# Attention scores from compact f16 halves in two 32-row passes per head, and a new order of steps

## The chip, the cores and the metric

The kernel runs on one core of a Trainium2 chip. The metric is the device time of one execution in microseconds; the median of 3 runs of the kernel before is 266.65 us (266.59 to 267.42).

## The reference

The input is 8 images of 256 tokens with 128 channels. Each image goes through a convolution-style attention layer, an attention layer with 8 heads of 16 channels, a small feed-forward layer and a mixture of 32 experts, of which each token uses two. The change touches the scores of the second layer. There queries, keys and values are all the same matrix `proj`:

```python
def _attn_quantum(h, theta):
    c = jnp.cos(h + theta)
    cp = jnp.cumprod(c, axis=-1)
    z0 = jnp.prod(c[..., 1:], axis=-1)
    return cp.at[..., 0].set(z0)

h = x.reshape(B, S, H, d)                      # 8 x 256 x 8 heads x 16
proj = _attn_quantum(h, theta_attn).transpose(0, 2, 1, 3)
scores = jnp.einsum('bhsd,bhtd->bhst', proj, proj) / jnp.sqrt(jnp.float32(d))
attn = jax.nn.softmax(scores, axis=-1)
ctx = jnp.einsum('bhst,bhtd->bhsd', attn, proj)
```

## The kernel before

One image is one batch `b` (0 to 7); its 256 tokens are two blocks of 128 partitions. All weights stay in the core's memory. The work of a batch is cut into 43 named steps in six chains: `conv` (first layer), `proj` (normalisation, angles, cosines, product scan, splitting), `attn`, `ffn`, `norm` and `moe`. Every engine runs its own part of each step in one common order, which `run_steps` (L387) makes by sorting a start offset per step (`START`) plus an offset per chain and batch (`CHAIN`). Within an engine all instructions run in that order; across engines they are tied by counting semaphores only. So a wait in one step holds back all later steps of that engine.

Eight banks of the accumulator memory hold matmul results, one for each purpose: `conv_ps`, `attn_ps`, two for the scores (`sc_ps`), `ffn_ps`, two for the hidden layer, `moe_ps`. `moe_transpose` of a batch waits until `moe_output` of the batch before has left `moe_ps` (`s_out_sb`); `attn_transpose` waits in the same way for `attn_combine` of the batch before (`s_z`).

The scores are made in f16 with f32 accuracy by splitting. `proj_split`: GpSimd writes `PA` (L1152, L1153), ScalarE casts it to f16, twice next to each other, as the high half of `LS` (L700), VectorE subtracts to get the low half, again twice (L899), and GpSimd copies both halves in another order to `RS` (L1158, L1160). Each head then has 64 values per token on either side: (high, high, low, low) against (high, low, high, low). `attn_transpose`: TensorE transposes `LS` in eight blocks of two heads into `attn_ps` (L492) and `RS` in eight blocks into bank 0 of the scores (L499); VectorE copies them out to `LT` (L907) and `RT` (two copies of 64 partitions, L912). `RT` has a zeroed half for the other head of a block, so that one matmul over 128 rows gives one head's scores. `attn_scores` of head h (L503 on): TensorE makes two matmuls of 256 columns into bank h % 2 (L509) once the exponential of head h-2 has been taken (`s_prob`); ScalarE takes the exponential of the 512 columns into `EB_` (L707). `attn_context` (L519) of four heads multiplies `EB_` with `PA`, each head writing its own 32 partitions of `attn_ps`.

## Time and profile before

| | |
|---|---|
| median of 3 runs | 266.65 us |
| span of the profiled execution | 265.1 us |
| TensorE busy | 193.9 us, 73% |
| VectorE busy | 174.5 us, 66% |
| ScalarE busy | 132.0 us, 50% |
| GpSimd busy | 126.3 us, 48% |
| mean granted TensorE clock | 0.955 |

The shares are averages over a pipeline that fills, runs full and empties; the stretches differ. The busy time of TensorE includes the ends of pipelined matmuls. The chain that ended last is followed back from the last instruction through what released it. PE is TensorE, PEld its weight loads, DVE VectorE, ACT ScalarE, POOL GpSimd. Except for loads at the start and 128 KB out per batch, nothing moves over DMA.

### The profile page before, as it was taken

To read this page: it belongs to the slowest core of one execution; us is meant where nothing else is said; L and a number is where in the kernel's file an instruction comes from. 1 tells how busy PE (TensorE), PEld (TensorE's weight loads), DVE (VectorE), ACT (ScalarE), POOL (GpSimd) and SP (SyncE) were. 2 spreads that over 40 slices of the span, in tenths; PEclk is the share of its full clock that TensorE was granted. 3 is DMA by queue.
4 is the path that set the end of the run, shared out by engine and by line. 5 is a ranking of instruction groups with operands and counts; after the bars stand their busy time and mean duration, and the time that the engine had idled before them with its cause. 6 is when DMAs were issued, how large, how long until landed. Compare 5 with 4: busy or idle time off the path is not lost.

```text
span 265.1 us, 4762 instructions
## 1 busy us (share of the span) xinstructions
PE 193.9 (73%) x1488; PEld 144.9 (55%) x1488; DVE 174.5 (66%) x580; ACT 132.0 (50%) x276; POOL 126.3 (48%) x321
## 2 busy tenths in 40 slices
PE   3372466649775667998899889859788868597395
PEld 2161253423662445786488668637666747476265
DVE  1333464776858788977888788698767566347323
ACT  2523537457458166646846673855447362412021
POOL 3706798265757568555744743376153161022100
PEclk9999999995979979999999999999999999979869
DMA  3385000000000000000000000000000000000000
GB/s 64 107 162 117 0 1 4 0 1 2 0 0 2 0 1 4 0 2 21 1 2 0 22 0 1 22 0 4 0 22 2 1 19 2 21 0 0 22 0 20
DMA packets 12624, 4.33 MB, mean 16 GB/s; under 512 B 6276, under 2 KB 12472, under 8 KB 12600
## 3 DMA queue, kind: packets, MB, share of 16 engines
q1 hardware_dynamic: 12104, 3.94, 6.4%
q8 instruction: 12, 0.20, 0.3%
q10 hardware_dynamic: 496, 0.09, 0.2%
q14 instruction: 12, 0.10, 0.1%
HBM read 2.98 MB, written 1.05 MB: 15 GB/s over the span
## 4 chain that ended last, share of the span: by engine, by line
PE 38%; DVE 29%; issue 10%; POOL 10%; ACT 9%; DMA 1%; ACTq 1%; POOLq 0%; DVEq 0%
PE hidden_ps L621 9%; PE moe_ps L606 6%; PE ffn_ps L570 4%; POOL rstd L1065 4%; DVE HWT L1007 3%; DVE RT L912 3%; DVE st L765 2%; PE sc_ps L509 2%; PE attn_ps L519 2%; PE hidden_ps L625 2%; PE conv_ps L476 2%; PE conv_ps L441 2%; ACT EB_ L707 1%; DMA bv_b<-in_L_conv_bv 1%; DVE ARG L877 1%
## 5 line engine op out<-in xcount | busy, mean ns | idle before, releaser
L707 ACT ACTIVATE EB_<-sc_ps 128x512 f32<-128x512 f32 x64 | 35.1, 597 | 15.1 <-PE sc_ps L509 14.3
L621 PE MATMUL hidden_ps<-XTT,keys_sb 128*128 128x256 f32 x128 | 40.8, 412 | 2.4 <-DVE HWT L1007 2.4
L747 ACT ACTIVATE HR<-hidden_ps 128x256 f32<-128x256 f32 x64 | 24.4, 384 | 35.7 <-PE hidden_ps L625 35.5
L606 PE MATMUL moe_ps<-val_sb,HWT 128*128 128x128 f32 x256 | 33.9, 277 | 2.6 <-DVE HWT L1007 2.6
L606 PEld LDWEIGHTS moe_ps<-val_sb,HWT 128*128 128x128 f32 x256 | 31.0, 192 | 6.6 <-DVE HWT L1007 3.5
L1007 DVE TENSOR_TENSOR HWT<-hidden_ps,HR 128x256 f32<-128x256 f32 x64 | 25.1, 418 | 12.1 <-ACT HR L747 10.3
L1063 POOL TENSOR_SCALAR var<-mv 128x2 f32<-128x2 f32 x32 | 6.6, 205 | 53.2 <-DVE mv L769 52.7
L509 PE MATMUL sc_ps<-RT,LT 128*128 128x256 f16 x128 | 22.9, 290 | 10.0 <-ACT EB_ L707 4.6
L621 PEld LDWEIGHTS hidden_ps<-XTT,keys_sb 128*128 128x128 f32 x128 | 20.6, 202 | 9.3 <-DVE HWT L1007 4.6
L1065 POOL TENSOR_TENSOR rstd<-var,minushalf 128x2 f32<-128x2 f32 x32 | 22.3, 697 | 2.7
L509 PEld LDWEIGHTS sc_ps<-RT,LT 128*128 128x128 f16 x128 | 10.7, 102 | 19.8 <-issue 13.6
L519 PE MATMUL attn_ps<-EB_,PA 128*32 128x256 f32 x256 | 18.1, 403 | 3.2 <-ACT EB_ L707 3.1
L570 PE MATMUL ffn_ps<-w2T_sb,HID 128*128 128x128 f32 x128 | 18.5, 306 | 2.3 <-ACT HID L730 2.3
L570 PEld LDWEIGHTS ffn_ps<-w2T_sb,HID 128*128 128x128 f32 x128 | 17.5, 219 | 3.0 <-ACT HID L730 2.9
L625 PE MATMUL hidden_ps<-WT,spread 96*128 96x256 f16 x64 | 18.1, 283 | 0.8 <-DVE WT L998 0.8
L730 ACT ACTIVATE HID<-ffn_ps 128x512 f32<-128x512 f32 x16 | 9.6, 598 | 8.9 <-PE ffn_ps L563 8.9
L683 ACT ACTIVATE EA<-conv_ps,nmx 128x256 f32<-128x256 f32 x16 | 7.4, 470 | 9.8 <-DVE nmx L836 9.7
L519 PEld LDWEIGHTS attn_ps<-EB_,PA 128*32 128x32 f32 x256 | 6.9, 113 | 9.8 <-ACT EB_ L707 5.6
L912 DVE COPY RT<-sc_ps 64x1024 f16<-64x1024 f16 x16 | 11.1, 694 | 0.3
L775 DVE TENSOR_SCALAR XTK<-T,mv,rstd 128x128 f32<-128x128 f32 x16 | 4.9, 345 | 9.2 <-POOL rstd L1065 9.2
L673 ACT COPY HW<-conv_ps 128x256 f32<-128x256 f32 x8 | 3.0, 372 | 16.0 <-DVE FGs L824 16.0
L476 PE MATMUL conv_ps<-HW,ETs 128*128 128x128 f32 x64 | 9.8, 300 | 1.4 <-DVE ETs L843 1.4
(174 smaller groups left out, 449.0 us busy)
## 6 DMA issues: line engine op xcount, KB each, us to landing
X<-in_x SPq DMA_DIRECT2D x8, 128.0 KB, 7.9
out<-OB SPq DMA_DIRECT2D x8, 128.0 KB, 1.8
keys_sb<-in_L_ffn_keys SPq DMA_DIRECT2D x1, 512.0 KB, 7.8
val_sb<-in_L_ffn_values SPq DMA_DIRECT2D x1, 512.0 KB, 9.0
w_sb<-in_L_attn_W SPq DMA_DIRECT2D x1, 256.0 KB, 2.8
g_b<-in_L_attn_ln_g SPq DMA_DIRECT2D x2, 64.0 KB, 5.5
be_b<-in_L_attn_ln_b SPq DMA_DIRECT2D x2, 64.0 KB, 6.5
bv_b<-in_L_conv_bv ACTq DMA_DIRECT2D x1, 64.0 KB, 3.6
```

The lines of the kernel that those rows point to most:

```text
L476: last = mm(conv_ps[:, t * C:(t + 1) * C], ETs[:, b % 2, m, t * P:(t + 1) * P], HW[:, b % 2, m, :], start=(m == 0), stop=(m == TB - 1))
L509: last = mm(sc_ps[h % 2][:, t * N:(t + 1) * N], LT[:, h // 2, t * P:(t + 1) * P], RT[:, h % 2, h // 2, :], start=True, stop=True)
L519: last = mm(attn_ps[32 * j:32 * j + 32, g * N:(g + 1) * N], PA[:, b % 2, t, h, :], EB_[:, h, t, :], start=(t == 0), stop=(t == TB - 1))
L570: last = mm(ffn_ps[:, t * C:(t + 1) * C], HID[:, k, t * P:(t + 1) * P], w2T_sb[:, k, :], start=(k == 0), stop=(k == FB - 1))
L606: last = mm(moe_ps[:, t * C:(t + 1) * C], HWT[:, k % 4, t * P:(t + 1) * P], val_sb[:, k, :], start=(k == 0 and t == 0), stop=(k == EB - 1) ...
L621: mm(hidden_ps[i][:, 0:N], keys_sb[:, k * EPB:(k + 1) * EPB, :].rearrange("p e h -> p (e h)"), XTT[:, b % 2, :], start=True, stop=True)
L625: mm(hidden_ps[i][:, N:2 * N], spread[:, k, :], WT[:, b % 2, :], start=True, stop=True).then_inc(s_moe_ps, 1)
L707: fn(EB_[:, h, :, :].rearrange("p t n -> p (t n)"), sc_ps[h % 2][:, :], ACT.Exp, scale=1.0 / math.sqrt(DK)).then_inc(s_prob, 1)
L747: fn(HR[:, k % 4, :], hidden_ps[i][:, 0:N], ACT.Relu).then_inc(s_relu, 1)
L912: V.tensor_copy(RT[q, i, :, :].rearrange("p j n -> p (j n)"), b16(sc_ps[0], F16)[q, :]).then_inc(s_RT, 1)
L1007: V.tensor_tensor(HWT[:, k % 4, :], hidden_ps[i][:, N:2 * N], HR[:, k % 4, :], ALU.mult).then_inc(s_hw, 1)
L1065: G.tensor_tensor(rstd[:, which, b, :], var[:, which, b, :], minushalf[:, :], ALU.pow).then_inc(rs, 1)
```

## The change

`LS` and `RS` become `HL` and `LH`: each head has (high, low) and (low, high), 32 values per token, with nothing held twice. ScalarE's cast and VectorE's subtraction write half as much; GpSimd makes `LH` from `HL` by one copy with the halves reversed. Four heads fit a transpose, so eight transposes make both sides, all into `attn_ps`; one copy brings them to `HLT`. `RT`, its zeros, its two copies and the use of score bank 0 for transposes are gone.

A head's scores are now two accumulated passes over 32 rows: (high, low) against (high, low), then (high, low) against (low, high). `attn_pair` handles two heads: its eight matmuls alternate between the heads, which lie in neighbouring groups of 32 rows and write to the two banks. The pair starts once both exponentials of the pair before are taken; the two heads' score semaphore steps come with the seventh and eighth matmul. The four products of halves (high-high, low-low, high-low, low-high) are the same as before.

`START` and `CHAIN` give way to `ORDER`, the place of each step and batch in a sequence of 312 steps. `moe_spread` counts one event less on `s_zeroed`.

```diff
--- before.py
+++ after.py
-START = {
-    "conv_transpose": 0.000, "conv_project": 0.131, "conv_stack": 0.478, "conv_scores": 0.664, "conv_turn": 0.991,
-    "conv_output": 1.190,
-    "proj_norm": 0.000, "proj_angle": 0.375, "proj_reduce": 0.557, "proj_cos": 0.794, "proj_split": 1.014,
-    "attn_transpose": 0.000, "attn_scores0": 0.123, "attn_scores1": 0.129, "attn_scores2": 0.267,
-    "attn_scores3": 0.295, "attn_context0": 0.465, "attn_scores4": 0.494, "attn_scores5": 0.508,
-    "attn_scores6": 0.552, "attn_scores7": 0.608, "attn_context1": 0.762, "attn_turn": 0.852, "attn_back": 1.085,
-    "attn_combine": 1.209,
-    "ffn_norm": 0.000, "ffn_angle": 0.372, "ffn_cos": 0.622, "ffn_transpose": 0.911, "ffn_hidden0": 1.301,
-    "ffn_hidden1": 1.545, "ffn_output": 1.730,
-    "norm_second": 0.000, "norm_third": 0.386,
-    "moe_transpose": 0.000, "moe_select": 0.095, "moe_topk": 0.125, "moe_spread": 0.395, "moe_pair0": 0.535,
-    "moe_pair1": 0.716, "moe_pair2": 0.998, "moe_pair3": 1.157, "moe_output": 1.189,
-}
-
-
-
-CHAIN = {
-    "conv": (0.000, 4.654, 5.883, 7.128, 8.599, 9.969, 11.330, 12.652),
-    "proj": (4.213, 6.104, 7.449, 8.826, 10.191, 11.562, 12.928, 14.505),
-    "attn": (5.828, 7.430, 8.902, 10.276, 11.607, 12.925, 14.284, 15.872),
-    "ffn": (7.444, 8.943, 10.284, 11.705, 13.063, 14.512, 16.131, 17.455),
-    "norm": (9.557, 10.883, 12.224, 14.018, 15.617, 16.569, 18.277, 19.630),
-    "moe": (10.535, 11.888, 13.236, 14.828, 16.048, 17.547, 18.900, 20.600),
+ORDER = {
+ORDER = {
+    "conv_transpose": (0, 8, 21, 38, 61, 85, 125, 163),
+    "conv_project": (1, 9, 22, 39, 66, 87, 128, 169),
+    "conv_stack": (2, 13, 27, 43, 71, 98, 136, 175),
+    "conv_scores": (3, 14, 28, 46, 72, 101, 139, 184),
+    "conv_turn": (4, 17, 31, 50, 75, 108, 148, 194),
+    "conv_output": (5, 19, 34, 55, 81, 110, 158, 199),
+    "proj_norm": (6, 20, 45, 56, 88, 111, 159, 208),
+    "proj_angle": (7, 26, 48, 69, 106, 115, 172, 214),
+    "proj_reduce": (10, 30, 54, 92, 117, 118, 188, 223),
+    "proj_cos": (11, 33, 59, 93, 121, 152, 196, 231),
+    "proj_split": (12, 37, 64, 99, 138, 167, 200, 234),
+    "attn_transpose": (15, 40, 68, 102, 143, 177, 205, 240),
+    "attn_pair0": (16, 41, 70, 103, 145, 181, 209, 245),
+    "attn_pair1": (18, 44, 77, 104, 154, 183, 212, 249),
+    "attn_context0": (23, 47, 78, 113, 160, 189, 215, 252),
+    "attn_pair2": (24, 49, 80, 114, 161, 190, 216, 253),
+    "attn_pair3": (25, 52, 82, 120, 164, 191, 218, 256),
+    "attn_context1": (29, 57, 86, 127, 168, 193, 220, 257),
+    "attn_turn": (32, 58, 89, 130, 170, 195, 225, 260),
+    "attn_back": (35, 62, 90, 135, 173, 198, 228, 266),
+    "attn_combine": (36, 63, 94, 137, 174, 202, 233, 268),
+    "ffn_norm": (42, 73, 105, 141, 186, 204, 237, 272),
+    "ffn_angle": (51, 79, 112, 146, 187, 224, 261, 276),
+    "ffn_cos": (53, 84, 123, 149, 201, 235, 263, 279),
+    "ffn_transpose": (60, 95, 129, 156, 210, 239, 269, 283),
+    "ffn_hidden0": (65, 97, 133, 180, 213, 243, 271, 288),
+    "ffn_hidden1": (67, 119, 134, 182, 222, 244, 277, 289),
+    "ffn_output": (74, 122, 150, 192, 229, 248, 278, 291),
+    "norm_second": (76, 126, 155, 207, 242, 250, 285, 292),
+    "norm_third": (83, 132, 165, 219, 246, 265, 287, 299),
+    "moe_transpose": (91, 142, 176, 221, 251, 273, 293, 303),
+    "moe_select": (96, 144, 178, 226, 254, 274, 294, 304),
+    "moe_topk": (100, 147, 179, 227, 255, 275, 295, 305),
+    "moe_spread": (107, 151, 185, 230, 258, 280, 296, 306),
+    "moe_pair0": (109, 153, 197, 232, 259, 281, 297, 307),
+    "moe_pair1": (116, 157, 203, 236, 262, 282, 298, 308),
+    "moe_pair2": (124, 162, 206, 238, 264, 284, 300, 309),
+    "moe_pair3": (131, 166, 211, 241, 267, 286, 301, 310),
+    "moe_output": (140, 171, 217, 247, 270, 290, 302, 311),
+}
...
-            for _, b, name in sorted((at + CHAIN[name.split("_")[0]][b], b, name)
-                                     for name, at in START.items() for b in range(NB)):
+            for _, b, name in sorted((at, b, name) for name, row in ORDER.items() for b, at in enumerate(row)):
...
-        LS = sb("LS", [P, 2, TB, H, 2, 2, DK], F16)
-        RS = sb("RS", [P, 2, TB, H, 2, 2, DK], F16)
-        LT = sb("LT", [P, H // 2, N], F16)
-        RT = sb("RT", [P, 2, H // 2, N], F16)
+        HL = sb("HL", [P, 2, TB, H, 2, DK], F16)
+        LH = sb("LH", [P, 2, TB, H, 2, DK], F16)
+        HLT = sb("HLT", [P, 2, H // 4, N], F16)
...
                     pe.wait_ge(s_rc, 1)
                 if b:
                     pe.wait_ge(s_z, b)
-                pe.wait_ge(s_left_l, b + 1)
-                pe.wait_ge(s_right, 2 * b + 2)
-                for j in range(H // 2):
-                    for t in range(TB):
-                        last = tr(b16(attn_ps, F16)[:, j * N + t * P:j * N + (t + 1) * P],
-                                  LS[:, b % 2, t, 2 * j:2 * j + 2].rearrange("p h i j d -> p (h i j d)"), identh[:, :])
-                last.then_inc(s_LT_ps, 1)
-                if b >= 1:
-                    pe.wait_ge(s_prob, H * b)
-                for j in range(H // 2):
-                    for t in range(TB):
-                        last = tr(b16(sc_ps[0], F16)[:, j * N + t * P:j * N + (t + 1) * P],
-                                  RS[:, b % 2, t, 2 * j:2 * j + 2].rearrange("p h i j d -> p (h i j d)"), identh[:, :])
-                last.then_inc(s_RT_ps, 1)
-
-            def attn_scores(b, h):
-                pe.wait_ge(s_RT, 2 * b + 2)
-                n = H * b + h
+                pe.wait_ge(s_hi, b + 1)
+                pe.wait_ge(s_lo, b + 1)
+                for side in range(2):
+                    if side:
+                        pe.wait_ge(s_lohi, b + 1)
+                    for g in range(H // 4):
+                        for t in range(TB):
+                            four = (HL, LH)[side][:, b % 2, t, 4 * g:4 * g + 4].rearrange("p h i d -> p (h i d)")
+                            at = (side * (H // 4) + g) * N + t * P
+                            last = tr(b16(attn_ps, F16)[:, at:at + P], four, identh[:, :])
+                last.then_inc(s_HLT_ps, 1)
+
+            def attn_pair(b, p):
+
+                pe.wait_ge(s_HLT, b + 1)
+                n = H * b + 2 * p
                 if n >= 2:
-                    pe.wait_ge(s_prob, n - 1)
-                for t in range(TB):
-                    last = mm(sc_ps[h % 2][:, t * N:(t + 1) * N], LT[:, h // 2, t * P:(t + 1) * P],
-                              RT[:, h % 2, h // 2, :], start=True, stop=True)
-                last.then_inc(s_score_ps, 1)
+                    pe.wait_ge(s_prob, n)
+                for t in range(TB):
+                    for side in range(2):
+                        for i in range(2):
+                            h = 2 * p + i
+                            j = slice(32 * (h % 4), 32 * (h % 4) + 32)
+                            last = mm(sc_ps[i][:, t * N:(t + 1) * N], HLT[j, 0, h // 4, t * P:(t + 1) * P],
+                                      HLT[j, side, h // 4, :], start=(side == 0), stop=(side == 1))
+                            if t == TB - 1 and side == 1:
+                                last.then_inc(s_score_ps, 1)
 
             def attn_context(b, g):
                 pe.wait_ge(s_prob, H * b + 4 * g + 4)
-                pe.wait_ge(s_LT, b + 1)
+                pe.wait_ge(s_HLT, b + 1)
...
                 if b >= 2:
-                    act.wait_ge(s_LT_ps, b - 1)
-                a = PA[:, b % 2].rearrange("p t h d -> p (t h) d")
-                l = LS[:, b % 2].rearrange("p t h i j d -> p (t h) i j d")
-                copy(l[:, :, 0], a[:, :, None, 0:DK].to_broadcast([P, TB * H, 2, DK])).then_inc(s_left_h, 1)
-
-            def attn_scores(b, h):
-                n = H * b + h
-                act.wait_ge(s_score_ps, n + 1)
-                if b >= 1:
-                    act.wait_ge(s_ctx_ps, 2 * (b - 1) + h // 4 + 1)
-                fn(EB_[:, h, :, :].rearrange("p t n -> p (t n)"), sc_ps[h % 2][:, :], ACT.Exp,
-                   scale=1.0 / math.sqrt(DK)).then_inc(s_prob, 1)
+                    act.wait_ge(s_HLT_ps, b - 1)
+                copy(HL[:, b % 2, :, :, 0].rearrange("p t h d -> p (t h) d"),
+                     PA[:, b % 2, :, :, 0:DK].rearrange("p t h d -> p (t h) d")).then_inc(s_hi, 1)
+
+            def attn_pair(b, p):
+                for i in range(2):
+                    h = 2 * p + i
+                    act.wait_ge(s_score_ps, H * b + h + 1)
+                    if b >= 1:
+                        act.wait_ge(s_ctx_ps, 2 * (b - 1) + h // 4 + 1)
+                    fn(EB_[:, h, :, :].rearrange("p t n -> p (t n)"), sc_ps[i][:, :], ACT.Exp,
+                       scale=1.0 / math.sqrt(DK)).then_inc(s_prob, 1)
...
-                dve.wait_ge(s_left_h, b + 1)
-                V.tensor_tensor(LS[:, b % 2, :, :, 1].rearrange("p t h j d -> p (t h) j d"),
-                                PA[:, b % 2, :, :, None, 0:DK].rearrange("p t h j d -> p (t h) j d").to_broadcast([P, TB * H, 2, DK]),
-                                LS[:, b % 2, :, :, 0].rearrange("p t h j d -> p (t h) j d"), ALU.subtract).then_inc(s_left_l, 1)
+                dve.wait_ge(s_hi, b + 1)
+                V.tensor_tensor(HL[:, b % 2, :, :, 1].rearrange("p t h d -> p (t h) d"),
+                                PA[:, b % 2, :, :, 0:DK].rearrange("p t h d -> p (t h) d"),
+                                HL[:, b % 2, :, :, 0].rearrange("p t h d -> p (t h) d"), ALU.subtract).then_inc(s_lo, 1)
 
             def attn_transpose(b):
-                dve.wait_ge(s_LT_ps, b + 1)
+                dve.wait_ge(s_HLT_ps, b + 1)
                 if b >= 1:
                     dve.wait_ge(s_score_ps, H * b)
-                V.tensor_copy(LT[:, :, :].rearrange("p j n -> p (j n)"), b16(attn_ps, F16)).then_inc(s_LT, 1)
-                dve.wait_ge(s_RT_ps, b + 1)
-                dve.wait_ge(s_zeroed, 1)
-                for i in range(2):
-                    q = slice(64 * i, 64 * i + 64)
-                    V.tensor_copy(RT[q, i, :, :].rearrange("p j n -> p (j n)"), b16(sc_ps[0], F16)[q, :]).then_inc(s_RT, 1)
+                V.tensor_copy(HLT[:, :, :, :].rearrange("p i g n -> p (i g n)"), b16(attn_ps, F16)).then_inc(s_HLT, 1)
...
-                G.memset(RT[:, :, :, :], 0.0).then_inc(s_zeroed, 1)
...
-                    pool.wait_ge(s_RT_ps, b - 1)
...
-                l = LS[:, b % 2].rearrange("p t h i j d -> p (t h) (i j d)").bitcast(U32).rearrange("p k (i j d) -> p k i j d", i=2, j=2)
-                r = RS[:, b % 2].rearrange("p t h i j d -> p (t h) (i j d)").bitcast(U32).rearrange("p k (i j d) -> p k i j d", i=2, j=2)
-                pool.wait_ge(s_left_h, b + 1)
-                G.tensor_copy(r[:, :, :, 0], l[:, :, 0]).then_inc(s_right, 1)
-                pool.wait_ge(s_left_l, b + 1)
-                G.tensor_copy(r[:, :, :, 1], l[:, :, 1]).then_inc(s_right, 1)
+                if b >= 2:
+                    pool.wait_ge(s_HLT_ps, b - 1)
+                pool.wait_ge(s_lo, b + 1)
+                hl = HL[:, b % 2].rearrange("p t h i d -> p (t h) (i d)").bitcast(U32).rearrange("p k (i d) -> p k i d", i=2)
+                lh = LH[:, b % 2].rearrange("p t h i d -> p (t h) (i d)").bitcast(U32).rearrange("p k (i d) -> p k i d", i=2)
+                G.tensor_copy(lh[:, :, :, :], hl[:, :, ::-1, :]).then_inc(s_lohi, 1)
```

## Rows read from the trace of the kernel before

**Rows 1.** Busy time by stretches (the columns are named in the first row).
```profile
core 0: us, PE busy (x) PEld busy (x) DVE busy (x) ACT busy (x) POOL busy (x), PEclk, DMA share, GB/s
...
100.00:120.00 20.00, 17.74 (x156) 13.60 (x154) 17.14 (x59) 11.50 (x28) 12.23 (x31) 1.00 0.01 2
...
120.00:140.00 20.00, 17.48 (x147) 13.16 (x148) 16.41 (x62) 11.91 (x28) 11.53 (x27) 1.00 0.03 8
...
160.00:180.00 20.00, 15.96 (x146) 12.14 (x144) 16.65 (x60) 11.46 (x22) 10.02 (x24) 1.00 0.03 7
...
240.00:265.00 25.00, 16.50 (x97) 12.56 (x95) 9.97 (x34) 5.10 (x14) 2.64 (x7) 0.86 0.04 11
```

**Rows 2.** Waits, 100 to 180 us: us in total, times, longest us.
```profile
DVE XTK L775 <- POOL rstd L1065: 3.4, 3, 1.2
...
PE moe_ps L597 <- POOL WP L1209: 2.8, 3, 1.7
```

**Rows 3.** Timeline of TensorE: start us, us, engine, line, what, count [idle before].
```profile
93.68 0.62 PE L492 MATMUL attn_ps<-identh,LS 128*128 128x128 f16 x8 [1.70 <-DVE Z L925]
...
98.08 0.64 PE L581 MATMUL moe_ps<-ident,XTK 128*128 128x128 f32 x2
...
123.19 0.44 PE L581 MATMUL moe_ps<-ident,XTK 128*128 128x128 f32 x2 [0.52 <-DVE OB L1013]
...
163.46 0.61 PE L492 MATMUL attn_ps<-identh,LS 128*128 128x128 f16 x8
...
211.18 0.44 PE L581 MATMUL moe_ps<-ident,XTK 128*128 128x128 f32 x2 [0.30 <-DVE OB L1013]
...
246.86 0.44 PE L581 MATMUL moe_ps<-ident,XTK 128*128 128x128 f32 x2 [0.52 <-DVE OB L1013]
```

**Rows 4.** The chain that ended last: shares by engine and line, then single pieces.
```profile
PE 38%; DVE 29%; issue 10%; POOL 10%; ACT 9%; DMA 1%; ACTq 1%; POOLq 0%; DVEq 0%
...
by line: issue 10.2%; PE hidden_ps L621 8.6%; PE moe_ps L606 6.2%; PE ffn_ps L570 3.8%; POOL rstd L1065 3.7%; DVE HWT L1007 3.3%; DVE RT L912 2.8%; DVE st L765 2.4%; PE sc_ps L509 2.3%; PE attn_ps L519 2.3%; PE hidden_ps L625 2.1%; PE conv_
...
28.58 0.63 ACT LS L700
...
94.94 0.67 DVE RT L912
...
164.07 0.45 PE sc_ps L499 x8
```

**Rows 5.** Groups of instructions: busy us, mean ns of one, idle before.
```profile
L912 DVE COPY RT<-sc_ps 64x1024 f16<-64x1024 f16 x16 | 11.1, 694 | 0.3
...
L899 DVE TENSOR_TENSOR LS<-PA,LS 128x512 f16<-128x512 f32 x8 | 5.9, 742 | 1.5 <-ACT LS L700 1.4
...
L925 DVE TENSOR_TENSOR Z<-attn_ps,YB 128x256 f32<-128x256 f32 x8 | 3.3, 418 | 0.9 <-PE attn_ps L542 0.9
...
L700 ACT CAST LS<-PA 128x512 f16<-128x512 f32 x8 | 4.9, 618 | 10.6 <-POOL PA L1153 10.6
...
L666 ACT COPY XT<-conv_ps 128x256 f32<-128x256 f32 x8 | 3.0, 372 | 9.6 <-PE conv_ps L432 9.6
...
L1160 POOL COPY RS<-LS 128x256 uint32<-128x256 uint32 x8 | 3.2, 399 | 3.1 <-DVE LS L899 3.1
...
L707 ACT ACTIVATE EB_<-sc_ps 128x512 f32<-128x512 f32 x64 | 35.1, 597 | 15.1 <-PE sc_ps L509 14.3
...
L509 PE MATMUL sc_ps<-RT,LT 128*128 128x256 f16 x128 | 22.9, 290 | 10.0 <-ACT EB_ L707 4.6 <-DVE RT L912 4.5
```

**Rows 6.** TensorE timeline, 101 to 106 us, and one piece of the chain.
```profile
101.85 1.07 PE L519 MATMUL attn_ps<-EB_,PA 128*32 128x256 f32 x16
...
102.85 0.61 PE L509 MATMUL sc_ps<-RT,LT 128*128 128x256 f16 x4
...
104.33 0.86 PE L509 MATMUL sc_ps<-RT,LT 128*128 128x256 f16 x4 [0.87 <-ACT EB_ L707]
...
114.60 0.43 PE hidden_ps L621 x2
```

More of the change, by code:

```diff
@@ L149, in build @@
         s_p_aug = sem("s_p_aug")
-        s_left_h = sem("s_left_h")
-        s_left_l = sem("s_left_l")
-        s_right = sem("s_right")
-        s_LT_ps = sem("s_LT_ps")
-        s_LT = sem("s_LT")
-        s_RT_ps = sem("s_RT_ps")
-        s_RT = sem("s_RT")
+        s_hi = sem("s_hi")
+        s_lo = sem("s_lo")
+        s_lohi = sem("s_lohi")
+        s_HLT_ps = sem("s_HLT_ps")
+        s_HLT = sem("s_HLT")
         s_score_ps = sem("s_score_ps")
@@ L593, in moe_spread @@
                 if b == 0:
-                    pe.wait_ge(s_zeroed, 2)
+                    pe.wait_ge(s_zeroed, 1)
                 pe.wait_ge(s_sel_e, b + 1)
@@ L634, in _ @@
                 "conv_scores": conv_scores, "conv_turn": conv_turn, "conv_output": conv_output,
-                "attn_transpose": attn_transpose, "attn_scores": attn_scores, "attn_context": attn_context,
+                "attn_transpose": attn_transpose, "attn_pair": attn_pair, "attn_context": attn_context,
                 "attn_turn": attn_turn, "attn_back": attn_back, "attn_combine": attn_combine,
@@ L751, in _ @@
                 "conv_output": conv_output, "proj_split": proj_split,
-                "proj_cos": proj_cos, "attn_scores": attn_scores, "attn_context": attn_context, "attn_back": attn_back,
+                "proj_cos": proj_cos, "attn_pair": attn_pair, "attn_context": attn_context, "attn_back": attn_back,
                 "ffn_cos": ffn_cos, "ffn_hidden": ffn_hidden, "moe_transpose": moe_transpose,
@@ L1153, in proj_split, with attn_pair @@
                 G.tensor_copy(a[:, :, 0:1], q[:, :, DK - 1:DK]).then_inc(s_p_aug, 1)
-                l = LS[:, b % 2].rearrange("p t h i j d -> p (t h) (i j d)").bitcast(U32).rearrange("p k (i j d) -> p k i j d", i=2, j=2)
-                r = RS[:, b % 2].rearrange("p t h i j d -> p (t h) (i j d)").bitcast(U32).rearrange("p k (i j d) -> p k i j d", i=2, j=2)
-                pool.wait_ge(s_left_h, b + 1)
-                G.tensor_copy(r[:, :, :, 0], l[:, :, 0]).then_inc(s_right, 1)
-                pool.wait_ge(s_left_l, b + 1)
-                G.tensor_copy(r[:, :, :, 1], l[:, :, 1]).then_inc(s_right, 1)
+                if b >= 2:
[4 more added lines that the diff above has]
+                G.tensor_copy(lh[:, :, :, :], hl[:, :, ::-1, :]).then_inc(s_lohi, 1)
                 if b == 0:
                     stack_w1()
-            def attn_scores(b, h):
-                if b == 0 and h == 0:
+            def attn_pair(b, p):
+                if b == 0 and p == 0:
                     set_moe_constants()
@@ L1212, in _ @@
                 "conv_project": conv_project, "conv_scores": conv_scores,
-                "proj_norm": proj_norm, "proj_angle": proj_angle, "proj_split": proj_split, "attn_scores": attn_scores,
+                "proj_norm": proj_norm, "proj_angle": proj_angle, "proj_split": proj_split, "attn_pair": attn_pair,
                 "ffn_norm": ffn_norm, "ffn_cos": ffn_cos,
```

## Prediction

> **What bounds the kernel now.** I read the busy shares first, by stretches of 20 us [rows 1]. The run has three parts. Up to about 100 us the pipeline fills and no engine is full. From 100 to 180 us VectorE is busy 82 to 86% of the time and TensorE 80 to 89% (four stretches, three of them shown). From about 211 us only feed-forward and mixture-of-experts (moe) steps are left, and VectorE falls to 40% in the last stretch while TensorE still has 66%.
>
> Second, who waits, over 100 to 180 us alone [rows 2]. The largest group of VectorE waits is 3.4 us, and its six groups together come to 10.3 us out of 80. TensorE's largest is 2.8 us, and its ten groups are 10.6 us. So here two engines are nearly full at once. Work taken from VectorE alone helps only until TensorE's own stream is bare: TensorE waits 10.6 us over the 3.45 batches of this stretch (one batch in 23.2 us, the spacing of the first attention transposes at 93.68 and 163.46 us in [rows 3]), or 3.1 us per batch.
>
> Third, the moe starts [rows 3]. Batch 0's is at 98.08 us, batch 1's at 123.19, batch 5's at 211.18, batch 7's at 246.86. They are serial, since each waits for the output of the one before. Batches 5 and 6 take 17.8 us each and batch 7 another 18.2, with no attention left, so the last 54 us hold nothing the change touches. What it saves must come before 211 us. There, one moe takes 25 us (98 to 123) because other steps sit between its own.
>
> Fourth, the chain that ended last [rows 4]: TensorE 38%, VectorE 29%, and the RT copy at L912 alone 2.8%, which is 7.4 us of 265.1. In time order it stands there eleven times, in six of the eight batches; the piece at 94.94 us is one.
>
> **The change part by part.** The profiled execution has a span of 265.1 us; its surroundings are worth 1.5 us, since the median of the runs is 266.65. I work on the span and add 1.5.
>
> *VectorE.* Gone are 16 RT copies of 64x1024 at 694 ns, 11.1 us [rows 5]. The LT copy stays as it is. The subtraction into LS has 256 elements in place of 512: from 742 ns to about 0.42 us, which is what L925 takes for 128x256 in f32. That is 0.32 x 8 = 2.6 us. VectorE loses 13.7 us of 174.5, 1.7 per batch.
>
> *ScalarE and GpSimd.* The cast goes from 512 to 256 elements, 618 ns to about 0.37 (L666, 128x256), 2 us in all. Of the two GpSimd copies (L1158 and L1160) one is left, with the same 256 words but with its halves reversed. The trace shows no reversed copy; I bound it by one and by two plain ones, 0.40 and 0.80 us, and take 0.45, near the plain one, since the words moved are the same. It needs only s_lo, as the second did. The memset of RT (1.8 us, once) is not on the chain and worth nothing.
>
> *TensorE, transposes.* 16 become 8. Eight take 0.45 us on the chain, so one is 56 ns: 0.45 us per batch saved, 3.6 in all. The second batch of them no longer needs bank sc0, thus no longer waits for the last exponential of the batch before.
>
> *TensorE, scores.* Per batch 16 matmuls of 128 rows become 32 of 32 rows, still 256 columns each. Now four in a row take 0.61 us [rows 6] and each 0.29 [rows 5], so they start 107 ns apart. What 32-row matmuls on alternating row groups do, this trace doesn't show. The nearest row is the context step, which puts four heads in four column groups: eight f32 matmuls (16 records) from 101.85 us to the next matmul at 102.85, 1.00 us, where one f32 matmul of the same 256 columns alone takes 0.43, so eight would take 3.44. Disjoint groups of the array therefore work side by side, 3.4 times over. By that the eight matmuls of a pair would cost two at a time, 4 x 107 = 0.43 us; their weight loads at the transposes' 56 ns make 8 x 56 = 0.45. That is what four matmuls cost today, so I take 0. Bounds: 0, and 16 x 107 = +1.7 us per batch if nothing overlaps. A gain is excluded, since the columns streamed two at a time are no fewer.
>
> *Changing the shape of the array.* In [rows 6] four column groups side by side need at least 3.44 / 4 = 0.86 us for what takes 1.00; the remaining 0.14 holds what leaving the context's layout costs, with uneven starts. I take 0.10 for a change, since most of it can be that; lower bound 0, upper bound 0.28, twice the rest, as the cost of entering is not in the row. Each pair now enters and leaves such a layout: up to 8 changes per batch, one of which exists already (context 0 to the scores behind it). 7 x 0.10 = 0.7 us per batch, 5.6 in all (0 to 15.7) against 3.6 saved on transposes. TensorE's own stream thus gets no shorter, about 2 us longer. The Trainium skill, page "TensorEngine Tiling (Array Packing)", section Key Properties, speaks against this change here: changing the tiling mode drains TensorE, while tiles of one mode run in parallel. The 0.14 us left over agrees with the first half, the context's 3.4 times with the second; neither row is of row tiles. Were a drain to cost the upper 0.28 each time, the sum below would carry 6.0 us in place of 2.1 and come to 264.7; with none it would be 258.7.
>
> *Scores waiting for both banks.* Before, head n waits for exponential n-2, so TensorE fills one bank while ScalarE reads the other. Now pair p waits for both exponentials of pair p-1 (1.2 us at 597 ns each, [rows 5]), and both exponentials wait for the pair's last matmuls. Today TensorE sits idle 4.6 us for exponentials ahead of scores in the whole run, 0.87 of it in one place [rows 5, 6]; there, with one exponential more to wait for, it would be about 1.5. Behind it on TensorE stands everything of the table. Between contexts a pair must find this twice per batch, 16 times. The new table puts other TensorE steps between them in 13 of the 16: only batch 3's pairs 0 and 1 and the pairs 2 and 3 of batches 0 and 5 are adjacent, and at two more places only a short step stands between (four stack transposes in batch 1, four selection matmuls in batch 7). Extra idle: 3 x 0.6 + 2 x 0.4 = 2.6 us; bounds 0 and 16 x 0.6 = 9.6.
>
> *Latency of the attention path.* From PA to the first score: cast -0.25, subtraction -0.32, two RT copies -1.4, and the second eight transposes ran under the LT copy. About 2 us sooner per batch. It is paid out only where this is what ends last.
>
> *The table.* It replaces a sum of two tables. Counting two heads as one step, there are 312 steps; moe_transpose of batch 0 is number 91 where it was 102, normalisation, angles and reduction of batch 5 move up 21 to 33 places, attention of batches 3 and 4 moves down by up to 13. From 211 us on the sequence has the same start (moe_transpose of batch 5 is number 273 in both). Nothing of the work changes by that. I give the earlier moe start 1.5 us (0 to 4), since that serial chain sets the end but the steps moved behind it must still be done.
>
> **The sum.** Chain terms that go: RT 7.4, one block of second transposes 0.45, one subtraction 0.32 and three casts at 0.25 each, together 8.9 us (first cast on the chain in [rows 4]; the subtraction stands right behind it). Next late is TensorE, whose waits of 3.1 us per batch can absorb 1.7 but not everywhere; I keep 7.5. Against it, array changes 5.6 x TensorE's chain share of 0.38 = 2.1, and pair waits 2.6, of which about 0.4 are on the path, 1.1. With the table: -7.5 + 2.1 + 1.1 - 1.5 = -5.8. Span 259.3, time 260.8 us, 2.2% faster.
>
> **The rivals.** *Row groups don't overlap.* For: no row shows them doing it, and both passes of a head accumulate in one bank. Against: the column groups do. It decides as soon as a pair takes 0.9 us in place of 0.45. Price: 1.7 us per batch, 14 in all, nearly all of it between 37 and 200 us, where TensorE has little or no slack from 100 us on; three quarters count, +10.5. 260.8 + 10.5 = 271.3, less what the covered waits give back (the later matmuls fall into waits already there), 270. Slower. Chance 0.10.
>
> *The bank handover is not covered.* For: interleaved steps are themselves often waiting (TensorE's waits are spread over ten groups in 100 to 180 us). Price: 9.6 us instead of 2.6, and array changes at their upper 0.28, 15.7 instead of 5.6; of 17 us more about half on the path, 8.5: 269.3, slower by 1.0%. It decides from about 6 us on the path. Chance 0.11.
>
> *VectorE's time is freed but TensorE was the bound.* For: TensorE at 87 to 89% from 100 to 140 us with a stream that becomes 2 us longer. Then only the filling part gains, about 2 us: 264.6. Chance 0.14 (a third of it within 0.3% of no change).
>
> *The savings come in full and the moe chain closes up.* The 2 us of latency count in each of eight batches in the part where no engine is full, and moe starts near 94 us: 13.7 us of VectorE time at two thirds, 9, plus 4 for the earlier start less 2: 11 us, 255.6. For: VectorE's waits in the middle are only 10.3 of 80 us. Chance 0.21.
>
> *The change doesn't do what it says* would mean pairs on two banks but RT-like copies left; the diff leaves none, and I give it nothing.
>
> **How the numbers follow.** Forecast (257.5 to 263.5) 0.41, full savings 0.21, partly absorbed 0.14, and around no change 0.03 from neighbours; uncovered handover 0.11, no overlap 0.10. A measurement of this kernel can tell about 0.3% from no change, 265.85 to 267.45. Faster: 0.41 + 0.21 + 0.10 = 0.72; same 0.04 + 0.03 = 0.07; slower 0.21. The range reaches from the middle of the full savings to the uncovered handover, 253 to 269.5; no overlap at all and savings beyond 13.7 us are left out, about 2 in 10.
>
> **What would show it.** Right: no RT group, VectorE near 161 us busy; eight score matmuls of a pair in 0.6 to 0.7 us (ends included); waits of the scores for EB_ below 8 us in total; moe starts before 98 us and again about 23 us apart or less until batch 4; the last three at 18 us as now. Wrong: a pair taking 1.0 us or more (no overlap), idle of 0.2 us or more around each pair without releaser (costly array changes), over 10 us of waits for EB_, or the last 54 us changed, which nothing here accounts for, unless TensorE's granted clock there (0.86 in the last stretch against 1.00 before [rows 1]) comes out another way.

## The result, and the profile after the change

The changed kernel takes 276.26 us (median of four, 275.94 to 281.96) against 266.62 us in the runs of the kernel before beside it: a ratio of 1.0342, 95% interval 1.0292 to 1.0392. The forecast was 260.8 us with a range to 269.5; the kernel became slower by 9.6 us (9.1 by the ratio), outside that range and in the other direction. Some executions of any of these kernels come out a few per cent longer at a lower granted clock (281.96 us at 0.829 here), and all ratios below compare the others. The profiled execution has a span of 274.1 us (before 265.1).

The page of the changed kernel: section 1 (busy time and share), then the lines of section 2 for TensorE and its granted clock, in tenths over 40 slices, then the first line of section 4 (the chain that ended last).

```profile
PE 208.3 (76%) x1552; PEld 149.6 (55%) x1552; DVE 160.7 (59%) x564; ACT 131.4 (48%) x276; POOL 119.4 (44%) x312
...
PE   3372687869667479986997799689869889659395
...
PEclk9999999975999957999999999989998979968959
...
PE 58%; DVE 14%; ACT 10%; issue 8%; POOL 7%; DMA 1%; ACTq 1%; POOLq 0%; DVEq 0%
```

VectorE has lost its 13.7 us (174.5 to 160.7). TensorE, which loses 64 transposes and has 256 score matmuls of 32 rows in place of 128 of 128 rows, is busy for 208.3 us where it was 193.9, and the chain goes 58% over TensorE and 14% over VectorE, where it was 38% and 29% [rows 4].

The new groups of the attention part, after; the columns are those of [rows 5].

```profile
L518 PE MATMUL sc_ps<-HLT 32*128 32x256 f16 x256 | 23.3, 308 | 11.5 <-ACT EB_ L717 6.1 <-DVE HLT L917 5.1
...
L917 DVE COPY HLT<-attn_ps 128x1024 f16<-128x1024 f16 x8 | 5.5, 688 | 1.7 <-PE attn_ps L504 1.6
...
L909 DVE TENSOR_TENSOR HL<-PA,HL 128x256 f16<-128x256 f32 x8 | 3.3, 417 | 1.8 <-ACT HL L708 1.7
L708 ACT CAST HL<-PA 128x256 f16<-128x256 f32 x8 | 3.2, 405 | 3.8 <-POOL PA L1156 3.8
L1163 POOL COPY LH<-HL 128x256 uint32<-128x256 uint32 x8 | 3.2, 400 | 10.6 <-DVE HL L909 10.6
```

Sixteen RT copies are gone, one HLT copy of 688 ns per batch is left, and the reversed copy at L1163 takes 400 ns. Scores wait 6.1 us for exponentials (4.6 before).

Starts of the moe batches after, on TensorE's timeline (columns as in [rows 3]; batches 0 to 4):

```profile
90.67 0.38 PE L591 MATMUL moe_ps<-ident,XTK 128*128 128x128 f32 x2
...
123.96 0.44 PE L591 MATMUL moe_ps<-ident,XTK 128*128 128x128 f32 x2 [0.52 <-DVE OB L1018]
146.83 0.39 PE L591 MATMUL moe_ps<-ident,XTK 128*128 128x128 f32 x2
179.07 0.69 PE L591 MATMUL moe_ps<-ident,XTK 128*128 128x128 f32 x2
199.36 0.44 PE L591 MATMUL moe_ps<-ident,XTK 128*128 128x128 f32 x2 [0.31 <-DVE OB L1018]
```

Batch 0 starts 7.4 us sooner than the 98.08 us of [rows 3], batch 1 already 0.8 us later, and batch 5, at 218.1 us, 6.9 us later. What comes behind it takes 56.0 us instead of 53.9. So the 9.0 us of span are lost at two places: 6.9 ahead of batch 5's start, 2.1 behind it.

For the first, busy time from 30 us to batch 5's moe start (stretch, length, then each engine with its count; the columns are named in [rows 1]), first the kernel before, then after:

```profile
30.00:211.20 181.20, 142.60 (x1209) 106.74 (x1209) 137.82 (x449) 104.46 (x221) 102.17 (x253) 0.96 0.02 4
```

```profile
30.00:218.10 188.10, 153.67 (x1265) 107.93 (x1265) 122.89 (x432) 103.30 (x220) 95.68 (x240) 0.93 0.01 4
```

TensorE's idle time fell from 38.6 to 34.4 us; its busy time grew by 11.1 us. VectorE lost 14.9 us of work and its idle time grew from 43.4 to 65.2 us. TensorE waits no longer than before: it takes longer over nearly the same work. TensorE's timelines say why. After, from 39 us:

```profile
39.34 1.94 PE L529 MATMUL attn_ps<-EB_,PA 128*32 128x256 f32 x16
...
43.51 1.03 PE L518 MATMUL sc_ps<-HLT 32*128 32x256 f16 x8 [1.27 <-ACT EB_ L717]
...
55.86 0.61 PE L518 MATMUL sc_ps<-HLT 32*128 32x256 f16 x8 [0.79 <-DVE HLT L917]
...
57.84 1.03 PE L518 MATMUL sc_ps<-HLT 32*128 32x256 f16 x8
```

and before, at the same time:

```profile
44.01 1.07 PE L519 MATMUL attn_ps<-EB_,PA 128*32 128x256 f32 x16 [0.47 <-ACT EB_ L707]
```

One context step takes 1.94 us or 1.07, one pair of heads 1.03 or 0.61: the same instructions at TensorE's lower level of clock (1.2 GHz) and at its upper (2.4 GHz). I counted runs of at least three matmuls that take over 1.2 times the short ones of their line. That is TensorE's time at the lower level: 50.0 us before and 89.3 us after. Before, the clock rises for the first time at 34.7 us, after at 51.2. After falls back at 57.8 to 68.2, 95.3 to 105.8, 177 to 181 and 205 to 208 us, and three times in the end; before has 59 to 65, 75 to 79 and 96 to 99, and two in the end. The granted-clock line above shows only part of this: it begins with the first recorded change of clock and reads 9 at 40 us, where the matmuls take double. Nor does its mean over a run rank the runs: the changed kernel took 276.19 us at a mean of 0.919, and 275.94 and 276.34 us at 0.869. Durations are the safer witness.

### The profile page after: what moved, and what is told of

The parts are those of the page before. It is cut to its first block, busy times and chain, and to the rows that moved or that the text cites. A ratio compares the mean times of both kernels' runs of the same rounds, so it can differ in the third digit from the quotient of the medians.

```text
span 274.1 us, 4833 instructions
## 1 busy us (share of the span) xinstructions
PE 208.3 (76%) x1552; PEld 149.6 (55%) x1552; DVE 160.7 (59%) x564; ACT 131.4 (48%) x276; POOL 119.4 (44%) x312
## 4 chain that ended last, share of the span: by engine, by line
PE 58%; DVE 14%; ACT 10%; issue 8%; POOL 7%; DMA 1%; ACTq 1%; POOLq 0%; DVEq 0%
PE hidden_ps L631 12%; PE moe_ps L616 8%; PE attn_ps L529 7%; PE sc_ps L518 7%; ACT EB_ L717 4%; PE conv_ps L483 4%; PE ffn_ps L580 3%; PE hidden_ps L635 3%; PE conv_ps L448 2%; POOL rstd L1069 2%; PE attn_ps L537 2%; PE attn_ps L552 1%; PE conv_ps L475 1%; DMA bv_b<-in_L_conv_bv 1%; DVE st L775 1%
## 5 line engine op out<-in xcount | busy, mean ns | idle before, releaser
L717 ACT ACTIVATE EB_<-sc_ps 128x512 f32<-128x512 f32 x64 | 34.7, 595 | 29.7 <-PE sc_ps L518 29.6
L631 PE MATMUL hidden_ps<-XTT,keys_sb 128*128 128x256 f32 x128 | 44.4, 442 | 0.8 <-DVE HWT L1012 0.8
L518 PE MATMUL sc_ps<-HLT 32*128 32x256 f16 x256 | 23.3, 308 | 11.5 <-ACT EB_ L717 6.1
L631 PEld LDWEIGHTS hidden_ps<-XTT,keys_sb 128*128 128x128 f32 x128 | 22.2, 217 | 8.2 <-DVE HWT L1012 3.5
L529 PE MATMUL attn_ps<-EB_,PA 128*32 128x256 f32 x256 | 21.9, 471 | 4.5 <-ACT EB_ L717 4.4
L518 PEld LDWEIGHTS sc_ps<-HLT 32*128 32x128 f16 x256 | 11.5, 101 | 22.4 <-issue 14.1
L580 PEld LDWEIGHTS ffn_ps<-w2T_sb,HID 128*128 128x128 f32 x128 | 15.9, 202 | 2.1 <-ACT HID L740 1.9
L483 PE MATMUL conv_ps<-HW,ETs 128*128 128x128 f32 x64 | 12.8, 365 | 0.8 <-DVE ETs L853 0.8
L1208 POOL TENSOR_TENSOR W<-SG,SR 128x64 f32<-128x64 f32 x8 | 2.6, 322 | 23.9 <-DVE SR L996 23.8
L483 PEld LDWEIGHTS conv_ps<-HW,ETs 128*128 128x128 f32 x64 | 11.5, 270 | 2.5 <-DVE ETs L853 2.0
L1155 POOL TENSOR_TENSOR PA<-SC,CS 128x240 f32<-128x240 f32 x8 | 4.9, 616 | 14.8 <-DVE SC L904 14.8
```

The source lines that it names most:

```text
L483: last = mm(conv_ps[:, t * C:(t + 1) * C], ETs[:, b % 2, m, t * P:(t + 1) * P], HW[:, b % 2, m, :], start=(m == 0), stop=(m == TB - 1))
L518: last = mm(sc_ps[i][:, t * N:(t + 1) * N], HLT[j, 0, h // 4, t * P:(t + 1) * P], HLT[j, side, h // 4, :], start=(side == 0), stop=(side = ...
L529: last = mm(attn_ps[32 * j:32 * j + 32, g * N:(g + 1) * N], PA[:, b % 2, t, h, :], EB_[:, h, t, :], start=(t == 0), stop=(t == TB - 1))
L580: last = mm(ffn_ps[:, t * C:(t + 1) * C], HID[:, k, t * P:(t + 1) * P], w2T_sb[:, k, :], start=(k == 0), stop=(k == FB - 1))
L631: mm(hidden_ps[i][:, 0:N], keys_sb[:, k * EPB:(k + 1) * EPB, :].rearrange("p e h -> p (e h)"), XTT[:, b % 2, :], start=True, stop=True)
L717: fn(EB_[:, h, :, :].rearrange("p t n -> p (t n)"), sc_ps[i][:, :], ACT.Exp, scale=1.0 / math.sqrt(DK)).then_inc(s_prob, 1)
```

## The experiments

The question was which part brings the lower clock, and whether the clock is the whole loss. In some kernels, extra matmuls are added whose result nobody reads. Ratios are to the kernel before, with 95% intervals.

**The scores without the table, and the table without the scores.** The first run keeps the new scores and goes back to the two old tables, a pair at the place of its first head (e1_new_scores_old_order) or of its second (e1_late_pairs_old_order). The second run puts the new table on the old kernel, a pair's two heads side by side.

```diff
-ORDER = { ... }
+START = { ..., "attn_pair0": 0.123, "attn_pair1": 0.267, "attn_pair2": 0.494, "attn_pair3": 0.552, ... }
+# late: 0.129, 0.295, 0.508, 0.608
+CHAIN = { ... }   # as before
```

> The changed kernel with the old START and CHAIN tables; pair p stands where head 2p stood. Theory A (the new table is what costs, the new scores are the gain I forecast): 259 to 264 us. Theory B (the 32-row pairs cost, through the bank handover, array changes or a lower granted clock, whatever the order): 273 to 278 us. If both share, about 268 to 270.

> The kernel before with the new ORDER, heads 2p and 2p+1 at pair p's place. Theory A: slower than before by 8 us or more, 275 to 285 (its VectorE has 13.7 us more to do than in the changed kernel). Theory B: 264 to 269, since the order is not what costs.

> As the run before, but pair p stands where head 2p+1 stood. It tells how far a place or two of the pairs matters. Theory A: within 2 us of the run before. If the handover of the two banks matters, more: pairs 0 and 1 are nearer to each other in the one than in the other, by up to 3 us.

Measured: new scores in the old order 1.0295 (1.0246 to 1.0345) at the early place, 1.0179 (1.0137 to 1.0221) at the late one; old scores in the new order 1.0220 (1.0171 to 1.0268). Each part alone slows the kernel. At the late place batch 0's moe starts at 100.8 us and batch 5's at 214.4. The two kernels of new scores have the same TensorE work up to 36 us, yet one got the upper clock at 34.8 us and the other not before 51. Contexts of e1_new_scores_old_order, then of e1_late_pairs_old_order:

```profile
39.90 1.07 PE L514 MATMUL attn_ps<-EB_,PA 128*32 128x256 f32 x16 [1.16 <-ACT EB_ L702]
```

```profile
41.34 1.94 PE L514 MATMUL attn_ps<-EB_,PA 128*32 128x256 f32 x16 [1.17 <-ACT EB_ L702]
```

So TensorE's work up to 36 us doesn't settle whether this rise comes.

**Is it the pairing?** e3 keeps the new operands and old order but runs head after head, each waiting for its own bank; e4 puts every head at exactly its old place as well.

```diff
-                n = H * b + 2 * p
-                if n >= 2:
-                    pe.wait_ge(s_prob, n)
-                for t in range(TB):
-                    for side in range(2):
-                        for i in range(2):
...
+                for i in range(2):
+                    h = 2 * p + i
+                    n = H * b + h
+                    if n >= 2:
+                        pe.wait_ge(s_prob, n - 1)
...
+                    for t in range(TB):
+                        for side in range(2):
```

> The changed kernel with the old tables, and each head on its own: four 32-row matmuls in one row group, waiting for the exponential two heads back as before. No matmuls overlap (a head would take 0.43 us of TensorE, a pair 0.86 in place of 0.43), but the two banks are handed over singly. If the overlap matters more: slower than the first run by 3 to 8 us. If the handover of both banks is the cost (a part of theory B): faster than it by 1 to 4 us.

> The new halves, transposes, single copy and 32-row passes, but each head by itself at exactly its old place in the old tables and with its old wait, four matmuls per head. It is the change without pairs and without the new table. Theory C (clock): it lands wherever its clock lands; with some 50 us at half clock as before, 260 to 264 us; with 75 to 90 us at half clock, as all variants so far had, 268 to 274. Theory B' (pairing, two exponentials waited for, is the cost): below 264 whatever the clock.

Measured: e3 1.0367 (1.0327 to 1.0406), e4 1.0108 (1.0015 to 1.0201). Without the double wait the scores wait 5.6 us for exponentials where the pairs at the same places (e1_new_scores_old_order) wait 12.1, yet e3 is no faster. It also has more time at the lower clock, 90 to 100 us (the count depends here on which durations are taken as the short ones) against 74 to 79, so this pair of runs doesn't separate the two. With every head at its old place the loss is about 1% (span 265.2, as before, with 65 us at the lower clock), and there is still no gain, though VectorE has lost its 13.7 us. By batch 5's moe start, 211.3 us as against 211.2 before, TensorE has been busy since 30 us for 152.6 us where it was 142.6.

**Is it the clock?** Five extra matmuls (128 columns, f16) ahead of TensorE's steps while the pipeline fills, until the first moe pair (not ahead of the attention transposes, and in batches 0 and 1 ahead of attention steps only); in three of the kernels also 30 after the selection of batches 5 to 7, in one those 30 alone.

```diff
+                for _ in range(5):
+                    mm(hidden_ps[1][:, 0:P], identh[:, :], identh[:, :], start=True, stop=True)
```

> The kernel before with extra matmuls that nobody reads: five of 128 columns ahead of each TensorE step while the pipeline fills (up to the first moe pair), thirty ahead of the wait for the expert weights in batches 5 to 7. Theory C (TensorE's clock is the term that was left out: 24 us at half clock before, 44 after): the granted clock rises above 0.97 and the time falls to 258 to 264 us, unless the extra matmuls stand in the way by more than they give. If the clock is a symptom only: 267 to 275.

> The changed kernel with the same extra matmuls. Theory C: clock above 0.96, time 260 to 267, so that the distance to the run before shrinks from 9.6 us to 4 or less. Theory A or B (the table or the handovers cost by themselves): 8 us or more above the run before.

> The changed kernel with the old tables, pairs at the place of the odd head, and the same extra matmuls. Theory C: its span with the loss at half clock taken off was 254.4 us, against 255.1 for the kernel before; so within 3 us of w1_before_busy, and 6 us or more below its own 271.7.

> The kernel before with the thirty extra matmuls in batches 5 to 7 alone. The stretches at half clock at 232 and 249 us cost it about 4 us of TensorE time in a serial chain. Theory C: 262 to 265 us. If the clock doesn't follow these matmuls: 266 to 268.

Measured: before 1.0231 (1.0131 to 1.0332); after 1.0129 (1.0054 to 1.0204), 5 us faster than the changed kernel without them; late pairs 1.0032 (0.9982 to 1.0082), where it had 1.0179. The kernel before with the 30 alone gave no usable ratio (267.35 to 274.58 us); in w1 the stretch behind batch 5's start took 58.8 us instead of 53.9, with 17.5 us at the lower clock where the kernel before had 8.5. So in that stretch the extra matmuls did not hold the clock up. The same useless work costs the old kernel 6 us and gives the new one 5: the time at the lower clock fell from 89.3 to 53.7 us in the new, and hardly in the old (50.0 to 48.4). The 30 cost more than they brought, so from here on only the filling was used.

**The parts compared at the same clock.** The five matmuls in the filling part alone, on four kernels. In f1 they stand ahead of all eight score steps of a batch, in g2 ahead of every other, as in f3, so that g2 and f3 carry the same filling.

> The kernel before with the five extra matmuls per TensorE step in the filling part alone; nothing extra at the end, where thirty per batch cost more than they gave. Its last 54 us should be as in the kernel before, so 264 to 267 us: it was already at full clock from 35 us on, apart from 13 us before 100 us.

> The changed kernel with the same. It ran at half clock from 19 to 50 us and from 58 to 68 us. Theory C: 268 to 271 us, 5 to 8 below the changed kernel; the rest of the distance to the kernel before is then the table and the later stretches at half clock. If the clock of the filling part doesn't matter: 274 to 277.

> The changed kernel with the old tables, pairs at the odd head's place, and the same. Theory C: 263 to 266 us, at or below the kernel before, since it had 30 us more at half clock and the last part gets its 54 us back. If the pairs by themselves cost: 268 or more.

> f1_before_fill with the extra matmuls ahead of every other score step only, so that they stand at the same 20 places per batch as in f3_late_pairs_fill (266.6 us). If the new scores are worth something once the clock is the same: 268 to 271 us, 2 to 4 above f3. If they are worth nothing: 265 to 267.

Measured:

| kernel, filled | ratio (95%) | at the lower clock | batch 5's moe start |
|---|---|---|---|
| old scores, old order, f1 | 1.0121 (1.0050 to 1.0193) | 41.8 us | 210.9 |
| the same, evenly, g2 | 1.0050 (1.0011 to 1.0088) | 44.5 us | 210.7 |
| new scores, old order, f3 | 0.9996 (0.9958 to 1.0034) | 34.9 us | 209.6 |
| new scores, new table, f2 | 1.0227 (1.0161 to 1.0292) | 65.0 us | 217.5 |

Read down, in us of 266.6: filling +1.3, new scores -1.4, new table +6.2; taking the filling out of the changed kernel +3.1; in all +9.1. The -1.4 is at the edge of what the intervals can tell, and each of the others carries 1 to 2 us of uncertainty. Busy time from 30 us to batch 5's moe start, in g2, f3 and f2:

```profile
30.00:210.70 180.70, 153.88 (x1489) 122.65 (x1489) 136.74 (x449) 104.86 (x221) 102.73 (x253) 0.99 0.02 4
```

```profile
30.00:209.60 179.60, 154.55 (x1553) 118.50 (x1553) 125.65 (x433) 102.64 (x221) 98.87 (x244) 0.97 0.02 5
```

```profile
30.00:217.50 187.50, 162.72 (x1525) 120.62 (x1522) 123.58 (x432) 103.00 (x220) 95.72 (x240) 0.94 0.02 4
```

From g2 to f3 VectorE loses 11.1 us of work and gains 10.0 us of idle time (44.0 to 54.0), while TensorE stays as busy and idles 25.1 us instead of 26.8. Over this stretch the two have the same time at the lower clock (10.5 and 10.2 us), so the comparison is a fair one. From f3 to f2 TensorE's idle time stays (25.1 and 24.8 us) and its busy time grows by 8.2 us, with some 20 filling matmuls fewer. Of this stretch f2 spends 32.1 us at the lower clock and f3 10.2. The 7.9 us by which batch 5's moe start is late thus lie in longer matmuls, not in waits.

**Where in the table?** h1 takes its first 110 steps from the new table and the rest from the old order, h2 the other way round; f5 is f2 with three extra matmuls ahead of each step between the moe batches too.

> The changed kernel with the first 110 steps in the order of the new table (to the first moe pair of batch 0) and the rest in the old order, pairs at the odd head's place, five extra matmuls per TensorE step in the filling part. If the new table loses in the middle only: moe starts near 88 us and the end comes at 260 to 265. If it loses by what its beginning leaves behind (the steps it put back): 268 to 274, as with the whole new table.

> The other way round: the first 110 steps in the old order, the rest in the new one, same extra matmuls. If the new table loses in the middle: 270 to 275. If it loses by its beginning: 264 to 268, as f3_late_pairs_fill (266.6).

> The changed kernel, five extra matmuls per TensorE step in the filling part as in f2_after_fill (273.8 us), and three ahead of each TensorE step between two moe batches up to batch 4. If the half clock in the middle (24 us in f2) is what costs, and these keep it away: 265 to 270 us. If its waits cost by themselves, or the extra work is not hidden: 273 to 277.

Measured: h1 1.0219 (1.0138 to 1.0301), h2 1.0509 (1.0440 to 1.0578), f5 1.0223 (1.0170 to 1.0277). The halves don't add up: each costs as much as the whole table or more, perhaps because steps around the seam get an order that neither table has. They settle nothing on the place. In f5 the time at the lower clock fell from 65.0 to 51.5 us and batch 5's moe started at 214.3 us in place of 217.5, but behind that start it took 55.8 us instead of 54.2, and by the ratios (1.0223 and 1.0227) nothing was gained. That the table's loss is its time at the lower clock is read from the traces and not confirmed by this run.

**Is it the missing transposes?** In the old kernel the clock rises right after two blocks of eight transposes. g1 is the late-pair kernel with eight unread ones put back per batch.

```diff
+                for g in range(8):
+                    four = HL[:, b % 2, g % 2, 0:4].rearrange("p h i d -> p (h i d)")
+                    tr(b16(attn_ps, F16)[:, g * P:(g + 1) * P], four, identh[:, :])
```

> e1_late_pairs_old_order (271.7 us) with eight transposes more per batch that nobody reads, ahead of the eight real ones: TensorE's work in this step is that of the kernel before. If the missing work is what leaves TensorE at half clock from 19 to 51 us: it rises near 35 us, 266 to 269 us, though 3.6 us of work is added. If the clock has nothing to do with it: 272 to 275 us.

Measured: 1.0107 (1.0060 to 1.0154), with single runs from 269.07 to 279.73 us. In the profiled execution the first context is still slow:

```profile
41.91 1.94 PE L517 MATMUL attn_ps<-EB_,PA 128*32 128x256 f32 x16 [1.18 <-ACT EB_ L705]
```

The theory that the transposes had kept the clock up falls for that run: the clock rose only near 52 us. That the ratio is better than the 1.0179 without them I can't explain. The profiled execution took 276.49 us, while the ratio rests on five runs of 269.07 to 272.02, so the trace may not speak for them, and whether the transposes matter stays open.

**A comparison that failed.** f4 is e4 with the filling.

> e4_heads_exact_old (single heads at their old places in the old tables) with the five extra matmuls in the filling part. Against f3_late_pairs_fill (266.6): within 2 us if pairs or heads make no difference once the clock is the same; 2 to 4 us faster if waiting for two exponentials costs.

Measured 1.0256 (1.0176 to 1.0335). With eight separate score steps the filling stands twice as often between exponentials that follow each other, as in f1, so it says nothing on the operands; g2 against f3 took its place.

## Why the prediction was wrong

**What bounds the kernel: right in kind, not carried through.** The prediction read two nearly full engines and said that VectorE's saving helps only until TensorE's stream is bare. It then kept 7.5 of 8.9 us, and for the new scores as a whole, with array changes and pair waits, forecast a gain of 4.3 us. g2 against f3 gives 1.4 us by the ratios and 1.5 by the spans: VectorE's time came free (11.1 us) and went into its own waits (10.0). The rival "VectorE's time is freed but TensorE was the bound" had this mechanism and nearly its size, a gain of 2 us. The step that failed here is the one from the chain of waits to the gain: the RT copies stood on the chain for 7.4 us, but TensorE, with 3.1 us of waits per batch, stood right behind. Between the forecast of -5.8 us and the +9.1 measured lie some 15 us. This step is 2.9 of them, the table is 7.7, and 4.4 are what the filling changes at its two ends (it costs the old kernel 1.3 and gives the new one 3.1).

**VectorE, ScalarE, GpSimd: right.** 160.7 us busy for a forecast of 161; subtraction 417 ns (0.42 forecast), cast 405 (370), reversed copy 400 (450).

**The pair of heads: right.** Eight 32-row matmuls take 0.61 us from the first start to the last end, as four 128-row ones do (0.60). The rival in which row groups don't overlap falls.

**Changes of the array's shape: right in size.** On TensorE's timeline, at the upper clock and with no wait between, before:

```profile
165.66 1.05 PE L606 MATMUL moe_ps<-val_sb,HWT 128*128 128x128 f32 x8
166.55 0.60 PE L509 MATMUL sc_ps<-RT,LT 128*128 128x256 f16 x4
166.99 1.06 PE L606 MATMUL moe_ps<-val_sb,HWT 128*128 128x128 f32 x8
```

and after:

```profile
169.75 1.05 PE L616 MATMUL moe_ps<-val_sb,HWT 128*128 128x128 f32 x8
170.74 0.61 PE L518 MATMUL sc_ps<-HLT 32*128 32x256 f16 x8
...
195.02 0.61 PE L518 MATMUL sc_ps<-HLT 32*128 32x256 f16 x8
195.56 1.16 PE L616 MATMUL moe_ps<-val_sb,HWT 128*128 128x128 f32 x8
```

From the start of the eight moe matmuls to the start of the scores it is 0.89 us before and 0.99 after. From the start of the scores to the start of the next step it is 0.44 and 0.54. Entering and leaving the 32-row layout thus cost about 0.10 us each, the forecast's figure. Only a context right ahead of a pair takes no longer than ahead of the old scores, 1.00 us on the chain:

```profile
105.91 1.00 PE attn_ps L529 x16
```

How much of these changes lies on the path (the sum's 2.1 us) no run separates: it is part of the 1.4 us net. The Trainium skill, page "TensorEngine Tiling (Array Packing)", section Key Properties, states a drain at each change of tiling mode. These rows agree with it.

**The handover of both banks: right.** 6.1 us of waits for exponentials against 4.6, inside the bound of 8. At the same clock it is 6.0 us in f3 against 2.2 in g2, and f3 is no slower for it. This rival falls too.

**The table: wrong sign, and the largest miss.** I gave it -1.5 us with bounds of 0 to 4 gained, and excluded a loss because "nothing of the work changes". Filled, it cost 6.2 us (f3 to f2); on the old scores 2.2%, 5.9 us. The moe of batch 0 did start before 98 us, as forecast. But batches 0 and 1 then lay 33.3 us apart and batches 2 and 3 32.2, where about 23 or less was forecast. The new sequence has 51 steps from moe_transpose of batch 0 to that of batch 1 (39 in the old order) and 45 from batch 2's to batch 3's (40 in the old), and part of the first ran at the lower clock (95.3 to 105.8 us). f2 against f3 shows the same two intervals, 33.5 and 34.0 us against 25.3 and 26.3. In f3 and f2 TensorE's waits are equal, and the loss is longer matmuls.

**The clock: the term that the sum lacked.** I treated the granted clock as a last caveat for the last 54 us. By the traces it is the largest item: 39 us more at the lower level. Between 30 us and batch 5's moe start that is most of the 11.1 us more busy time (the new operands are 0.7 of it by g2 and f3), against which 4.2 us of idle time went. In the end part, which the prediction left untouched, it stands beside the 2.1 us lost: 16.4 us at the lower level there, 8.5 before. The Trainium skill, page "TensorE: Matmul & The Clock Gate", section "What's actually happening", puts the penalty of the ramp under 1% of a typical kernel's span and says that the ramp varies from run to run. The variation agrees: four runs of the changed kernel show mean granted clocks of 0.829 to 0.919. The size is not this kernel's: TensorE, in short bursts between waits, falls back to the lower level seven times after its first rise and spends 89.3 of 274.1 us there.

**What stays open.** Why the new table leaves TensorE longer at the lower clock in the middle, and what decides whether the first rise comes at 35 or at 51 us. The filling shows that more work on TensorE brings the clock back early in the run (in the changed kernel the first rise moves from 51.2 to 37.8 us, while the thirty matmuls at the end of w1 did not help) and that the new scores then lose nothing; it doesn't show which gap loses it. No version here beats the kernel before: f3, new scores in the old order with filling, ties with it.

## What to carry to other kernels

Where the matrix engine waits often, look at its clock before anything else: list the stretches where the same instruction takes twice as long, and ask of each saving or move ahead of a stretch whether it thins the engine's work there. A saving on the chain of waits is worth only the slack of the next engine behind it; subtract that engine's own busy time from the stretch before keeping any of it. A new order of the same steps is not free: give it a loss as well as a gain, and look at what lands between two links of the serial chain.

## What the hardware showed that was not expected

In e3 the program has head A's four 32-row matmuls first and then head B's four, on another row group. Two pieces of its TensorE timeline:

```profile
152.09 0.62 PE L503 MATMUL sc_ps<-HLT 32*128 32x256 f16 x8
...
175.28 1.00 PE L503 MATMUL sc_ps<-HLT 32*128 32x256 f16 x8
```

With both banks free the eight take 0.62 us, as when the program alternates between the groups. So head B's matmuls run beside head A's although all of A's stand ahead in the program; their recorded starts lie 0.014 us apart. Where head B had to wait for its bank, the group takes 1.00 us: there B's first matmul starts 0.40 us behind A's, 0.06 us after the exponential that frees its bank has ended.
